# Last feed-forward of a two-layer gated cross-attention block: the first bias as gathered rows, added by VectorE, in place of a product with one-hot rows

## What is computed

```
idx = argmax(softmax(x @ gate_w + gate_b, axis=1), axis=-1)
for e in range(8):
    h = gelu(x @ W1[e] + b1[e])        # 128 -> 512
    y = h @ W2[e] + b2[e]              # 512 -> 128
    out = out + where(idx == e, y, 0)
```

## Time and profile before

| | us |
|---|---|
| median of 3 runs | 723.8 |
| lowest and highest | 723.74, 726.2 |
| profiled execution, its own time | 723.51 |
| its span in the profile | 721.8 |

### The profile page before, as it was taken

How to read it: one execution, slowest core, us unless ns; L and a number is a source line. 1 busy time by engine, 2 the same in 40 slices (tenths; PEclk the granted TensorE clock), 3 DMA queues, 4 the chain that set the end, 5 groups by cost and what they waited for, 6 DMA issues and landing times.

```text
span 721.8 us, 14356 instructions
## 1 busy us (share of the span) xinstructions
PE 657.7 (91%) x5392; PEld 494.1 (68%) x5392; DVE 526.0 (73%) x1074; ACT 374.6 (52%) x581; POOL 354.0 (49%) x450
## 2 busy tenths in 40 slices
PE   5878999999989988999999999999999999787994
PEld 4755666666778776776777767776777776566884
DVE  4667788676598887797767877868798877565533
ACT  3656766765543354545554555545454455425552
POOL 3185444450034422576676667657576466760131
PEclk9879999999999999999999999999999999999998
DMA  8200000000300003000000000102000002100212
GB/s 186 23 0 2 2 2 1 3 2 1 120 2 1 0 1 110 2 1 2 1 5 27 16 2 16 30 2 59 3 2 1 2 1 60 43 27 16 63 47 57
DMA packets 35268, 16.97 MB, mean 24 GB/s; under 512 B 12824, under 2 KB 33648, under 8 KB 35072
## 3 DMA queue, kind: packets, MB, share of 16 engines
q1 hardware_dynamic: 33680, 14.94, 7.9%
q0 software_dynamic: 512, 1.05, 0.5%
q10 hardware_dynamic: 1008, 0.07, 0.1%
HBM read 12.05 MB, written 3.93 MB: 22 GB/s over the span
## 4 chain that ended last, share of the span: by engine, by line
PE 67%; DVE 20%; issue 7%; POOL 2%; ACT 2%; DMA 1%; SPq 0%; POOLq 0%; DVEq 0%; ACTq 0%
PE ps L1934 63%; DVE o L1635 3%; DVE pmax L1622 2%; PE ps L1945 2%; DVE mx L1305 2%; DVE kql L1610 1%; DVE exm L1501 1%; DVE pmax L1619 1%; POOL y_tok L725 1%; POOL xs_scratch L717 1%; PE ps L2038 1%; DMA raw<-in_L_xattn_Wproj_dram 1%; PE ps L2583 1%; DVE wsel L1498 0%; DVE rt_y L1412 0%
## 5 line engine op out<-in xcount | busy, mean ns | idle before, releaser
L1014 ACT ACTIVATE p<-ps 128x1024 f32<-128x1024 f32 x96 | 96.5, 1025 | 151.1 <-PE ps L1934 151.1
L751 POOL TENSOR_TENSOR acc<-p 128x256 f32<-128x256 f32 x128 | 94.9, 773 | 74.2 <-ACT p L1014 74.1
L1934 PE MATMUL ps<-p,v 128*64 128x256 f32 (+1 forms) x1280 | 123.4, 384 | 0.8 <-DVE xr L1331 0.5
L1934 PE MATMUL ps<-kqh 64*128 64x256 f32 (+1 forms) x640 | 111.0, 374 | 13.6 <-DVE pmax L1619 4.0
L757 POOL TENSOR_TENSOR acc<-acc,p 128x256 f32<-128x256 f32 x128 | 91.8, 749 | 54.1 <-ACT p L1014 54.0
L1619 DVE TENSOR_REDUCE pmax<-ps 128x2 f32<-128x1024 f32 x64 | 78.2, 1221 | 33.5 <-PE ps L1934 33.3
L1305 DVE TENSOR_REDUCE mx<-ps 128x1 bf16<-128x512 f32 x128 | 82.4, 687 | 26.5 <-PE ps L1934 25.9
L1934 PEld LDWEIGHTS ps<-p,v 128*64 128x64 f32 (+1 forms) x1280 | 66.1, 126 | 46.7 <-issue 15.2
L1934 PEld LDWEIGHTS ps<-kqh 64*128 64x128 f32 x640 | 62.4, 193 | 43.1 <-issue 34.4
L654 POOL TENSOR_SCALAR q<-qst,rmask 128x256 fp32r<-128x256 f32 x64 | 58.8, 938 | 59.1 <-ACT qst L774 59.1
L878 ACT ACTIVATE p<-ps 128x1024 f32<-128x1024 f32 x64 | 65.5, 1025 | 23.1 <-PE ps L1934 21.4
(11 more groups left out here) (318 smaller groups left out, 1437.7 us busy)
## 6 DMA issues: line engine op xcount, KB each, us to landing
w_raw<-in_L_ffn_W_dram SPq DMA_DIRECT2D x8, 256.0 KB, 2.6
ys_scratch<-y SPq DMA_DIRECT2D x22, 64.0 KB, 1.5
ctx_all<-in_ctx_dram SPq DMA_DIRECT2D x4, 256.0 KB, 5.5
raw_kv<-in_L_xattn_Wkv_dram SPq DMA_DIRECT2D x1, 1024.0 KB, 4.9
ctx_all<-in_L_ffn_W_dram SPq DMA_DIRECT2D x4, 256.0 KB, 3.6
w_raw_late<-in_L_ffn_W_dram SPq DMA_DIRECT2D x4, 256.0 KB, 3.8
xs_scratch<-xnA SPq DMA_DIRECT2D x1, 832.0 KB, 4.5
xs_rawA<-xs_scratch SPq DMA_DIRECT2D x3, 256.0 KB, 3.4
```

The lines of the kernel that those rows point to most:

```text
L751: ins = pool.tensor_tensor(acc1[:, at], p1[:, s, 0, at], p1[:, s, 1, at], ALU.add)
L1014: act.activation(p1[:, g % 2, u, :], bank(2 * (n % 2), 2), ACT.Exp, scale=SCALE1).then_inc(a_exp1.sem, 1)
L1934: return pe.matmul(o, lhsT, rhs, start=start, stop=stop)
```

## The change

The fourth product of `up1` is dropped. Before a tile's gelu, VectorE now adds a bias row to the PSUM bank and writes the sum to SBUF (`biased`), and ScalarE takes its gelu from there. The rows come from `b1` in DRAM by an indirect DMA on GpSimd for each tile (`b1_in`), which fetches the row of the tile's expert of set z for each of the 128 partitions. They go into six buffers, two groups of up to three tiles; there are eight groups: tile 0, then 1-3, 4-6, 7-9, 10-12, 13-15, 16-18 and 19-21. A group's gathers wait until the gelus of the group two before are done. An up bank is free again after `biased` and not after the gelu. `xs_h` and `xs_l` become rings of 12 tiles to make room, and the bias tables shrink to b2's part. The second layer's bias product stays, so `hot` is still needed there.

```diff
@@ gpsimd
+            def b1_in(k):
+                lo, hi = B1_GROUPS[k]
+                z = int(lo >= SLOT_TILES[0])
+                pool.wait_ge(d_route.sem, d_route.after(z, 5))
+                if k == 0:
+                    pool.wait_ge(e_pv1.sem, e_pv1.after(G1 - 1, 0))
+                    pool.wait_ge(g_fold.sem, G1 - 1)
+                if k >= 2:
+                    pool.wait_ge(a_gelu.sem, B1_GROUPS[k - 2][1])
+                for tile in range(lo, hi):
+                    t = tile - z * SLOT_TILES[0]
+                    pool.indirect_dma_start(
+                        out=b1_row(tile), out_offset=None, in_=t_in["L1_ffn_b1"],
+                        in_offset=bass.IndirectOffsetOnAxis(ap=expert_i[z][:, t:t + 1], axis=0)
+                        ).then_inc(s_b1[k % 2].sem, 16)
...
                 ins.then_inc(g_acc.sem, 1)
+                if g == G1 - 1:
+                    b1_in(0)
                 pool.wait_ge(a_exp1.sem, a_exp1.after(g, 3))
...
+            b1_in(1)
             spread_hot(0)
+            b1_in(2)
+            b1_in(3)
             scattered(1, xnB3, range(TOKEN_TILES[1]))
+            b1_in(4)
             spread_hot(1)
+            for k in range(5, len(B1_GROUPS)):
+                b1_in(k)
             gathered(0)
             gathered(1)
@@ scalar
             def gelu(tile):
-                act.wait_ge(e_up.sem, tile + 1)
+                act.wait_ge(d_pre.sem, tile + 1)
...
-                act.activation(hid1[:, tile % 2, :], bank(UP_BANK[tile % 2]), ACT.Gelu).then_inc(a_gelu.sem, 1)
+                act.activation(hid1[:, tile % 2, :], b1_row(tile), ACT.Gelu).then_inc(a_gelu.sem, 1)
@@ vector
+            def biased(tile):
+                k = b1_group(tile)
+                dve.wait_ge(e_up.sem, tile + 1)
+                dve.wait_ge(s_b1[k % 2].sem, 16 * sum(hi - lo for lo, hi in B1_GROUPS[k % 2:k + 1:2]))
+                dve.tensor_tensor(b1_row(tile), bank(UP_BANK[tile % 2]), b1_row(tile), ALU.add).then_inc(d_pre.sem, 1)
...
             slots_low(0)
             divide1(G1 - 1)
+            biased(0)
             for tile in range(SLOTS_ALL):
+                if tile + 1 < SLOTS_ALL:
+                    biased(tile + 1)
@@ tensor
                     pe.wait_ge(d_xsL.sem, k + 1)
                     pe.wait_ge(g_hot.sem, k + 1)
                 if tile >= 2:
-                    pe.wait_ge(a_gelu.sem, tile - 1)
+                    pe.wait_ge(d_pre.sem, tile - 1)
...
-                mm(o, xs_l[:, tile, :], of_expert(w1_h), False, False)
-                mm(o, hot[:, tile, :], biases_hl[:, 0:F], False, True).then_inc(e_up.sem, 1)
+                mm(o, xs_l[:, tile % XS_RING, :], of_expert(w1_h), False, True).then_inc(e_up.sem, 1)
```

44 lines of the change are left out of this document (31 added, 13 removed).

## The result

| | before | after |
|---|---|---|
| median, us (6 runs each) | 723.89 | 744.23 |
| lowest and highest | 721.92, 726.2 | 740.21, 745.56 |
| profiled execution, its own time | 723.51 | 740.21 |
| its span | 721.8 | 738.5 |

The ratio is 1.0279, with a 95% interval of 1.025 to 1.0308: some 20 us slower, where 15.2 were forecast. The direction and most of the sum held; the forecast of 738.9 is 5.3 us too low, and the measured time lies above its range of 731 to 743.

The account below looks back on a forecast made before the run. The bound was to move from TensorE to a ring through VectorE and ScalarE. Terms 3.0 + 1.55 + 3.7 - 0.4 + 1.3 + 1.65 + 4.1 + 0.3 = 15.2 us gave 738.9 us, range 731 to 743 with two neighbouring rivals.

Parts of the forecast that it names:

- The ring through VectorE and ScalarE: Last feed-forward: bias addition, gelu, copy, hidT_l and output addition wait on each other in a loop, 2.68 us a turn.
- H(8): H(t) is the start of tile t's subtraction hidT_l on VectorE; for tile 8 forecast at 686.7.
- The rival that TensorE stays the bound: Last feed-forward: each removed product counts and the kernel gets faster, 718.7 to 720.5 us; chance 3%.
- The start: First pass +3.0 us, behind three gathers and GpSimd's cast; from there to tile 0's hidT_l +1.55.
- tiles 1 and 2: Additions stand behind VectorE's last residual and normalisation, so hidT_l of each tile comes 1.86 us later, 3.7 together.
- half speed: First two passes taken at half clock after TensorE's idle time: 1.0 of the 1.55 us before tile 0's hidT_l.
- inside this: The three gathered tiles land at about 650, within the time before tile 0's hidT_l at 653.0.
- Tiles 2 to 8: Routing stretch: -0.4 us for tiles 2 to 5, +1.3 for tiles 5 to 8.
- The late gather of tile 10: Bias rows of tiles 10 to 12, gathered after the last scatters, land in 3.2 us and delay the addition: +1.65 us.
- From H(9) on: Later tiles to the last output: ring turns, low halves and residual additions; +4.1 us was forecast for tiles 8 to 21.
- the residual gather's 0.3: Gather of batch results follows the last bias gather and lands at about 719.2, the first residual addition due 718.9: +0.3 us.
- The rival that GpSimd is shut out: Gather at 636.6 finishes only after VectorE's w2_low subtractions, everything behind slips up to 4.4 us: 743.3 us; chance 6%.

Follow-up runs that it names:

- first profile: Profiled execution of the changed kernel without any edit, 740.21 us, the quickest of its six.
- one-row kernel with filler: One-row kernel plus four products of 256 columns per tile whose results nobody reads: 732.95 us, 1.0168 of the kernel before.
- one-row kernel: Changed kernel with only tile 0's bias row gathered and added to every tile, 21 gathers left out: 738.36 us, 1.0234 of the kernel before.
- filler: Changed kernel plus four products of 256 columns per tile whose results nobody reads, also tried in other kernels: 744.36 us, 1.0276 of the kernel before.
- second profile: Profile of an execution of 743.86 us of the changed kernel, run again without any edit.
- later wait for the cast: Changed kernel with TensorE's wait for GpSimd's cast moved from the first layer's pass to the second layer's products: 742.57 us, 1.0288 of the kernel before.
- opened one-row kernel: One-row kernel with ScalarE's copy of tile t put before the gelu of tile t+1: 725.19 us, 1.004 of the kernel before.
- group 4 first: Changed kernel with the bias gathers of tiles 10 to 12 put ahead of the last sequence's scatters: 737.52 us, 1.0232 of the kernel before.
- the base: The changed kernel run again without any edit: 743.84 us, 1.0306 of the kernel before.
- the three moves: Changed kernel with cast wait at the second layer, ScalarE's copy before the next gelu, tiles 10 to 12 gathered before the scatters: 731.55 us, 1.014.
- the ceiling: Kernel before without the first layer's bias product, nothing in its place: 720.34 us, 0.9977 of the kernel before.

## Why the prediction was right in its mechanism and wrong in its size

**The ring through VectorE and ScalarE: right.** Forecast 2.68 us a turn, measured 2.67, and the steps with something extra came out too: in the first profile the step to tile 12 takes 4.51 (forecast 4.5; 5.11 in the second) and the one from tile 18, with a residual and a low half, 3.83 (3.8). With no late gather and the clock up, in the one-row kernel with filler, the whole piece from H(8) to the last output takes 39.9 us, against 39.5 forecast. Turning ScalarE's order opens it, and with no gather in the way that is worth 13.2 us. The rival that TensorE stays the bound fell.

**The start, 4.55 in sum, and tiles 1 and 2: the size right, the reason only in part.** By the second profile 4.59, then 2.00 and 1.85 where 1.86 was forecast for each: the first pass is 3.03 late (forecast 3.0), and from there to H(0) it takes 4.84 (4.8). The half speed in that working was my estimate from the 0.53 of the earlier trace rows, behind a gap of 3.7 us; behind the wait ahead of the first pass the granted clock is 0.54 from 646 to 649 in the second profile, 0.55 and 0.50 from 643 to 649 in the first, and 1.00 from 643 to 649 in the kernel with the later wait for the cast, whose first pass starts at 643.32. One step of the working does not add up: six products at half clock cost 6 x 0.23 = 1.4 us more, not 1.0, and without it 0.2 would be left of the 1.55, not 0.5; the sum is not touched. And the cast was only one of three gates that close within 3 us of each other: it, the landing of gathers 1 to 3 (2.70 us of wait once the cast's gate is gone), and the reciprocal on VectorE in front of the first additions (1.1 us in the one-row kernel). There 1.3 more came from a slow stretch of TensorE ahead of the stage (granted clock 0.68), which not every execution has: the same 24 products took 2.81 us in the first profile, at 1.00, and 4.96 in the second, at 0.56. So how late H(0) is without the cast's gate depends on the execution too. My working named only the first gate, and said that the three tiles land "inside this". Taking the gate away that I named gave 1.3 us, not clear of the noise, and not 3.0.

**Tiles 2 to 8: +0.9 in sum forecast, +3.4 measured in the second profile, 2.5 too little.** I counted half clock for the first two passes and full clock after. The granted clock was 0.66 from 660 to 680 us there; with filler, at 0.91, the piece from H(2) to H(8) takes 24.4 us instead of 26.25, 1.8 less. So this step failed by the clock for the most part; 0.7 us stay at the higher clock, and no run takes them apart. In the first profile this piece cost 1.5.

**The late gather of tile 10: the step that failed most.** I forecast 1.65 over a turn that is 0.3 longer, 1.95 from H(8) to H(9); the second profile has 5.12, **3.2 more**, the first 4.61, 2.7 more. I had taken a landing of 3.2 us, between 2.6 and 3.8. A gather of 128 rows of 2 KB landed after 4.1 us in the median, outside my bounds, and up to 6.7 at this place, where the load of `xs_rawB` and three more gathers share the DMA engines (busy 1.12 and 357 GB/s in the row of the second profile). My price came from places where the DMA engines moved less: 23 and 44 GB/s in the two stretches of 3 us around the last gathers of y in the kernel before. No gather of a bias row here landed in under 3.7 us. The wait is 2.24 with the load held back. With the group ahead of the scatters it is gone, and the kernel 6.3 us faster.

**From H(9) on: 4.1 forecast (the residual gather's 0.3 in it), 5.4 in the second profile, 6.6 in the first.** The step from H(10) to H(11) is 3.45 and 3.44 in place of 2.67, both in or just behind a half-clock stretch (0.51 from 691 to 694 us in the first, 0.50 from 697 to 700 in the second), and in the first profile the last tile falls into another (0.50 from 727 to 730), 1.7 us.

These are the 7.1 us between 15.2 and 22.34: 2.5, 3.2, 1.3 and 0.1. In the first profile, where 20.12 was reached, the same four are 0.7, 2.7, 2.5 and -0.9: the gather's term is the largest miss in both. The second profile reached the stage 1.85 us earlier than the profile of before, and what remains is the 5.3 by which the median was missed.

**What of the clock is shown.** That low clock costs time in a kernel with the ring is shown in the one-row kernel: more products, the granted clock from 0.83, 0.74 and 0.83 to 1.00, 0.91 and 1.00, and 5.4 us less. That the ring alone brings it about is not: the opened one-row kernel has a mean clock of 0.967, against 0.961 with the ring closed, and the kernel before has 0.977. It is not shown that it costs as much in the changed kernel itself: the filler raised the clock, gained 2.0 us up to tile 8, lost 0.7 of them in the step with tile 10's addition, and moved the median by nothing that the runs can tell. That time gained ahead of tile 10 is spent waiting for a gather whose issue hangs on the routing was only argued; with group 4 first, where that wait is gone, the filler gained nothing in the median either, and why it does in the one-row kernel and not there stays open. By the profiles the stage got shorter with filler every time, by 4.5 us in the one-row kernel and by 1.2 to 2.5 in the other three, which one profile of each cannot tell from none.

**The rival that GpSimd is shut out: fell.** The gather at 633.24 ran beside VectorE's subtractions with two SBUF inputs and kept GpSimd for 1.36 us instead of 0.95, in the second profile for 0.99; nothing slipped by 4.4. That the gather could finish only behind the subtractions, from which the 743.3 follows, was a supposition that no row of the kernel before shows, and in the runs the gather lost 0.4 us at most. What did get in each other's way are the additions and the subtractions: 2.77 and 6.58 us in the first profile, 4.24 and 4.62 in the second.

**What it adds up to.** From the base's 743.84, without 21 gathers 738.36 (-5.5), with the ring opened too 725.19 (-13.2), and without any addition 720.34 (-4.9). In the ring the filler takes 5.4 us off and opening it 13.2; the two are not parts of one sum, since the opened kernel has stretches at half clock as well (0.50 from 661 to 664 us and from 679 to 685). No complete version of the change beats the kernel before: the three moves are 1.4% slower, with filler 0.9%, and the ceiling is 1.2 us.

**Left open.** What fills the landing up to 5.3 us once the load is gone: the six gathers issued within some 7 us around it are likely companions, which was not tried. Open too is why executions of one kernel have their half-clock stretches at different places; the two profiles of the changed kernel do (from 661 to 667 us the granted clock is 1.00 in the first, 0.50 and 0.54 in the second), and their stages differ by 2.2 us.

## What to carry to other kernels

Idle time on an engine is room for an operation only if the operation's place in that engine's order does not close a loop: write down who waits for whom over one turn, add the durations, and compare with the bound of today. TensorE's waits can cost more than their own length: the ring of 2.67 over a bound of 2.16 is 11 us in 22 tiles at most, and closing it cost 13.2; with filler products in those waits the one-row kernel took 5.4 us less, at a granted clock of 0.91 to 1.00 in place of 0.74 to 0.83. And before moving a small product off the busiest engine, take it out and measure: here that one run gives a ceiling of 1.2 us in the median, while the products' own times add up to 5.1.

What a move is worth depends on the wait behind it: the same turned order gave 2.8 us with the gathers in place, and 13.2 without them. And a price for a transfer read where the DMA engines are little used can be too low where others share them: 3.2 us was taken from places with 23 and 44 GB/s, and in the first profile, with 342 GB/s from 685 to 688, a landing took up to 6.7.
